# Value rounds issued in pairs, with fifteen probability slots, in a two-block transformer kernel

## What is computed

```
q = q * cos + rotate_half(q) * sin
k = k * cos + rotate_half(k) * sin
scores = einsum('bhgtd,bhkd->bhgtk', qg, k) / sqrt(16)
scores = where(causal, scores, min)
attn = softmax(scores)
ctx = einsum('bhgtk,bhkd->bhgtd', attn, v)
```

## Time and profile before

| | |
|---|---|
| median of three runs | 753.19 us |
| the profiled execution | 752.28 us |
| its span, first to last instruction | 750.5 us |
| TensorE (PE) busy | 707.6 us, 94% |
| VectorE (DVE) busy | 480.8 us, 64% |
| ScalarE (ACT) busy | 314.7 us, 42% |
| GpSimd (POOL) busy | 313.8 us, 42% |
| heads 0 to 7 of the attention | 84.9 to 324 us |

### The profile page before, as it was taken

One profiled execution on the slowest core, in us unless ns is written; L12 is line 12 of the kernel. 1 busy time (PEld: TensorE's weight loads), 2 busy tenths in 40 slices (PEclk: granted clock), 3 DMA queues, 4 the chain that ended last, 5 costly groups with the idle time before them and its releaser, 6 DMA issues.

```text
span 750.5 us, 10313 instructions
## 1 busy us (share of the span) xinstructions
PE 707.6 (94%) x3718; PEld 429.5 (57%) x3718; DVE 480.8 (64%) x722; ACT 314.7 (42%) x530; POOL 313.8 (42%) x254
## 2 busy tenths in 40 slices
PE   4998899999999998999999999999789999999998
PEld 1444343334333332366778888555357888877886
DVE  3787778788888887439675468768785432337211
ACT  3311367677676667732335211554243323223100
POOL 0325673866665568803366233216422212216300
PEclk9999999999999999999999999999889999999999
DMA  8347516264171100120133100231010111012111
GB/s 301 116 127 223 125 44 166 74 123 72 55 190 35 24 3 2 61 76 23 29 84 98 43 1 0 81 66 48 29 41 0 57 56 56 28 57 63 36 70 43
DMA packets 24111, 53.00 MB, mean 71 GB/s; under 512 B 4252, under 2 KB 8100, under 8 KB 23044
## 3 DMA queue, kind: packets, MB, share of 16 engines
q1 hardware_dynamic: 24068, 52.44, 25.1%
HBM read 45.63 MB, written 6.60 MB: 70 GB/s over the span
## 4 chain that ended last, share of the span: by engine, by line
PE 75%; DVE 14%; issue 5%; POOL 2%; DMA 2%; SPq 1%; ACT 1%; DVEq 0%; POOLq 0%; ACTq 0%
PE ps L895 72%; DVE mxp L1869 3%; DVE st L1711 1%; DMA rq<-in_mask 1%; PE ps L912 1%; DVE xnb L1735 1%; DVE x L1956 1%; DVE x L2069 1%; PE ps L1081 1%; DVE rt L1750 1%; POOL pr L2310 1%; DVE dg L2103 0%; ACT pr L1516 0%; PE ps L1088 0%; DVE qsw L1920 0%
## 5 line engine op out<-in xcount | busy, mean ns | idle before, releaser
L895 PE MATMUL ps<-arena 128*128 128x512 f32 (+1 forms) x1404 | 327.2, 392 | 1.2 <-POOL arena L2416 0.5
L895 PEld LDWEIGHTS ps<-arena 128*128 128x128 f32 (+1 forms) x1404 | 259.9, 186 | 60.8 <-issue 1.7
L1869 DVE TENSOR_REDUCE mxp<-ps 128x2 f32<-128x1024 f32 (+3 forms) x160 | 172.5, 1114 | 40.2 <-PE ps L895 39.6
L1516 ACT ACTIVATE pr<-ps 128x512 f32<-128x512 f32 x288 | 161.3, 597 | 73.7 <-PE ps L895 69.7
L895 PE MATMUL ps<-Kst,Qst 96*128 96x512 bf16 (+3 forms) x384 | 97.0, 330 | 5.4 <-DVE mxp L1869 4.2
L895 PE MATMUL ps<-Qst,Kst 99*128 99x512 bf16 x288 | 96.1, 385 | 1.8 <-ACT pr L1516 1.4
L2310 POOL TENSOR_TENSOR pr<-pr,cap 128x512 int32<-128x512 int32 x56 | 70.2, 1269 | 38.4 <-ACT pr L1516 38.4
L895 PE MATMUL ps<-pr,vr 128*32 128x512 f32 x576 | 76.7, 604 | 1.4 <-POOL pr L2310 1.4
L895 PEld LDWEIGHTS ps<-Kst,Qst 96*128 96x128 bf16 x384 | 35.8, 98 | 50.6 <-DVE mxp L1869 20.9
L895 PEld LDWEIGHTS ps<-Qst,Kst 99*128 99x128 bf16 x288 | 24.6, 97 | 64.3 <-ACT pr L1516 45.8
L2416 POOL TENSOR_TENSOR arena<-raw,arena 128x1024 fp32r<-128x1024 f32 x11 | 26.7, 2431 | 80.1 <-ACT arena L1589 80.1
(11 more groups left out here) (205 smaller groups left out, 842.6 us busy)
## 6 DMA issues: line engine op xcount, KB each, us to landing
wmr<-in_wmr SPq DMA_DIRECT2D x8, 1280.0 KB, 11.1
raw<-in_w SPq DMA_DIRECT2D x16, 512.0 KB, 3.3
Qst<-q_parts SPq DMA_DIRECT2D x42, 128.0 KB
q_parts<-qparts SPq DMA_DIRECT2D x3, 768.0 KB, 4.6
x<-in_x SPq DMA_DIRECT2D x8, 256.0 KB, 5.9
wm<-in_wm SPq DMA_DIRECT2D x4, 512.0 KB, 7.3
raw<-in_up SPq DMA_DIRECT2D x8, 256.0 KB, 2.6
raw<-in_down SPq DMA_DIRECT2D x8, 256.0 KB, 2.5
```

The costliest lines, as they stand in the source:

```text
L895: return nc.tensor.matmul(outp, lhs, rhs, start=start, stop=stop, skip_group_check=True)
L1516: A(pr[:, k % PRING, :], ps[:, t_bank(n, k), :], ACT.Exp, scale=float(DH) ** -0.5).then_inc(exp_done, 1)
L1869: V.tensor_reduce(mxp[:, kh, g0:g0 + heads, i].rearrange("p (b e) -> p b e", e=per), units, AXX, ALU.max)\
```

## The change

In heads 0 to 6 the rounds 0 to 7 are issued two at a time: rounds 0 and 1 behind unit 11, 2 and 3 behind 19, 4 and 5 behind 27, 6 and 7 behind 35. Round 8 stays behind unit 1 of the next head. The last head keeps its order. The places of all units, score units, `max_turn`, `mod_step` and `ctx_turn` in the list stay as they are.

The ring gets 15 slots (13 in head 0, because slots 13 and 14 lie where the third rotary piece of the queries is read until head 0). A table says which slot each unit uses and which unit used it before; each exponential waits for the round of that unit. The first exponential of head 1 also waits for `part_q` to reach 3, the end of the rotary work. `ot` stays where it was.

```diff
-PRING = 12
-assert NTU % PRING == 0 and NTU == 4 * ROUNDS
+PRING = 15
+assert NTU == 4 * ROUNDS
+FIRST_PRING = 13
+def ring_table():
+    slots, held, user = {}, {}, {}
+    for n in range(NKV):
+        for k in range(NTU):
+            s = k % FIRST_PRING if n == 0 else (NTU + (n - 1) * NTU + k - NTU // FIRST_PRING * FIRST_PRING) % PRING
+            slots[n, k], user[n, k] = s, held.get(s)
+            held[s] = n * NTU + k
+    return slots, user
+PSLOT, PUSER = ring_table()
...
-        pr = at("pr", [P, PRING, D], F32, HT_B)
-        ot = at("ot", [P, 2, D], F32, HT_B + PRING * 2048)
+        pr = [at(f"pr{s}", [P, D], F32, HT_B + 2048 * s) for s in range(12)]
+        pr += [at("pr12", [P, D], F32, WR_B + 12800), at("pr13", [P, D], F32, ACT_B + 76 * 1024),
+               at("pr14", [P, D], F32, ACT_B + 78 * 1024)]
+        ot = at("ot", [P, 2, D], F32, HT_B + 12 * 2048)
...
                     t_unit(n, k)
-                    if k % 4 == 3 and k > 4:
-                        pv_round(n, k // 4 - 1)
+                    if k % 8 == 3 and k > 4:
+                        for r in range(2):
+                            pv_round(n, k // 4 - 2 + r)
                     if k == 1 and n:
                         pv_round(n - 1, ROUNDS - 1)
...
                     act.wait_ge(t_full, n * NTU + k + 1)
-                    if k >= PRING or n:
-                        act.wait_ge(pv_done, n * ROUNDS + (k - PRING) // 4 + 1)
-                    A(pr[:, k % PRING, :], ps[:, t_bank(n, k), :], ACT.Exp, scale=float(DH) ** -0.5).then_inc(exp_done, 1)
+                    if n == 1 and k == 0:
+                        act.wait_ge(part_q, 3)
+                    if PUSER[n, k] is not None:
+                        act.wait_ge(pv_done, PUSER[n, k] // 4 + 1)
+                    A(pr[PSLOT[n, k]][:, :], ps[:, t_bank(n, k), :], ACT.Exp, scale=float(DH) ** -0.5).then_inc(exp_done, 1)
```

More of the change, by code:

```diff
@@ L1069, in pv_round @@
                     q = 32 * strip(i)
-                    last = mm(ps[q:q + 32, 6 + i // 4, :], vr[:, j, :], pr[:, k % PRING, :], j == FIRST_J[i],
+                    last = mm(ps[q:q + 32, 6 + i // 4, :], vr[:, j, :], pr[PSLOT[n, k]][:, :], j == FIRST_J[i],
                               j == LAST_J[i])
@@ L2308, in mask_round @@
                     pool.wait_ge(exp_done, n * NTU + k + 1)
-                    v = pr[:, k % PRING, :].rearrange("p (g t) -> p g t", g=G).bitcast(I32)
+                    v = pr[PSLOT[n, k]][:, :].rearrange("p (g t) -> p g t", g=G).bitcast(I32)
                     nc.gpsimd.tensor_tensor(v, v, cap[:, :].unsqueeze(1).to_broadcast([P, G, P]), ALU.mult).then_inc(masked, 1)
```

## The result

| | before | after |
|---|---|---|
| median, five runs each | 753.19 us (752.57 to 754.71) | 767.08 us (764.77 to 767.47) |
| ratio | | 1.018, 95% interval 1.016 to 1.020 |
| the profiled execution | 752.28 us | 766.93 us |
| its span | 750.5 us | 765.1 us |

The change makes the kernel 13.9 us slower. The forecast was 768.5 us, its range 762.5 to 773.

The account below looks back on a forecast made before the run. TensorE bounds, busy 94% of the span. Head 0 +3.4, heads 1 to 4 +8.8, head 5 +1.3, head 6 +1.8 sum to +15.3 us: 768.5 us on the median of 753.19, range 762.5 to 773.

Parts of the forecast that it names:

- its rivals: Only the border saved, 748.4 us, 5%; no change, 3%; VectorE waits hidden, 757.2, 7%; border saves nothing, 773.3, 10%.
- The new waits: Behind units 7, 15, 23 and 31 TensorE waits 0.63, 0.56, 1.10 and 0.60 us: 2.89 in a head.
- The border: Between a pair's two rounds TensorE saves 0.17 us, 0.68 in a head, 4.8 over 28 pairs.
- The rival in which the border saves nothing: The second round of a pair waits for its weights or the first to drain: 773.3 us, chance 10%.
- Head 0: First head: +1.8 us from waits less borders, plus 1.6 for `nm` held by GpSimd, together +3.4.
- The hold: In head 0 `nm` would start inside a GpSimd operation and end with it: +1.6 us, bounds 0 and 1.6.
- two precedents: In the earlier traces a CAST (107.77 to 109.09) and an `nm` of 1.00 us each ended with GpSimd's operation.
- its rule: Trainium skill: GpSimd shares SBUF interfaces with VectorE, and instructions with two SBUF inputs contend there; gives head 0's 1.6 us.
- The stall of 0.81: Head 5's context transposes wait for VectorE; the pair before nearly removes this, -0.9 us, so head 5 costs +1.3.
- Head 6: Costs +1.8 us: 2.21, less 0.20 for the wait behind unit 31, less 0.25 for GpSimd's effect on `nm`.
- the 0.81 of the earlier trace: In head 6 `max_turn` loses 0.81 us to GpSimd before the change; forecast change -0.8 to +0.3, taken as -0.25.
- The edits at nothing: Ring slots, GpSimd masks, the wait on `part_q`, value copies and DMAs were claimed to cost no time.

Follow-up runs that it names:

- One place given back: Changed kernel with round 4 back behind unit 23 and round 5 behind 27, three pairs left in heads 0 to 6: 760.0 us, ratio 1.0088.
- Work put into the places: Changed kernel with three more matmuls of 512 columns behind units 7, 15, 23 and 31 of heads 0 to 6: 767.73 us, ratio 1.0193.
- the run without the GpSimd hold: Changed kernel with GpSimd's last 1024-column rotary operation cut into four of 256 columns: 766.34 us, ratio 1.0189.
- The run with 12 slots: Kernel before, with its ring of 12 slots, and its rounds issued in pairs: 765.65 us, ratio 1.0168.
- the run with the ring alone: Changed kernel with its table of 15 slots, but single rounds behind every fourth unit as before: 753.11 us, ratio 0.9999.
- Half the reductions: Kernels before and after, VectorE's score reductions reading half of the columns, exponentials at scale 0: 743.57 us (from before) and 751.99 us (from after).
- the second: Changed kernel with VectorE's score reductions over half of the columns and exponentials at scale 0: 751.99 us, ratio 0.9986.

## Why the prediction was right

**The mechanism.** It was the one forecast: in four places of each head TensorE comes 1.09 us sooner to work that isn't ready. The experiments separate it from its rivals. The ring is free. The pairs make the loss without it. One place given back returns its own price. Work put into the places is nearly free. The part that the experiments don't settle is the fall of the clock in head 0, 1.4 of the 14.7 us.

**The new waits.** In head 3 the forecast had unit 8 0.41 behind unit 7 and unit 9 0.66 behind that; the rows say 0.42 and 0.65. The score unit behind unit 15 was to be 0.56 late; it is 0.57, at 201.01 and so 0.79 behind unit 15 at 200.22, where 0.22 would do. At units 24, 25 and the transpose the sum was 1.10 and is 1.10, and the transpose stands 1.85 behind unit 23, as said. Behind unit 31 it was 0.60, and is 0.60 (215.16 is 0.82 behind 214.34). With 0.05 us for every release, read off one place of the chain, no wait is off by more than 0.02.

**The border.** Here a size was off. The forecast took 0.17, the way out of one round and into the next, and called it the most, "since a strip's passes can't overlap themselves". It is 2.09 - 1.86 = 0.23. The 0.17 wasn't the most: what the sum left out is that the passes of the second round come 0.43 behind each other where the second pass of a single round comes 0.46 behind the first (0.45 at 197.25). Over 28 pairs that is 6.5 in place of 4.8 us. The rival in which the border saves nothing is excluded. This term alone takes 1.7 us off the forecast, and the middle heads, 1.97 in place of 2.21, are off by just it.

**Head 0.** By its own terms it comes to 1.8 - 0.24 of more border = 1.56, and the run without the GpSimd hold has 1.55. The hold was to cost 1.6 and costs 1.93 - 0.19 = 1.74: `nm` started at 107.20, forecast at 107.22. That makes 3.3. The other 1.4 of the 4.67 was not forecast: it is the fall of the clock behind the idle 2.13 us. The run with 12 slots has the hold, 1.31 of it, and no fall: +2.81, and 1.55 + 1.31 is 2.86. The forecast priced a wait by its length. It left out that the clock can fall at a long one. That the idle time is the cause isn't shown. With the hold, two profiled runs in which TensorE idled for 2.07 and 2.13 us have the fall, and four in which it idled for 0.77 to 1.70 don't; but the clock fell in head 6 of another run without such a gap. The forecast also took two precedents for the hold, and only `nm` has the two SBUF inputs that its rule names: the CAST reads one tile.

**Head 5.** The stall of 0.81 is gone, and the head costs 1.13: 1.97 - 0.81 = 1.16.

**Head 6.** Forecast 1.8, measured 0.93. `nm` there is back to 0.19, at 305.65, so the 0.81 of the earlier trace rows came back in full; the forecast had taken the middle of -0.8 and +0.3. The wait behind unit 31, estimated at 0.4, is 0.37, so 1.97 - 0.23 - 0.81 gives 0.93. The lower end of the bounds was right, by little: `nm` started 0.07 ahead of the next GpSimd operation (305.72). In the run with GpSimd's operation in quarters, whose head 6 has the same list, a lower clock took back more than this.

**The sum.** 1.7 less by the border and 0.6 less by head 6 stand against 1.4 more by the clock in head 0: 15.3 against 14.67 us. That the total came so near owes something to this cancelling; without the clock's part it would have been 13.3 and 766.5 us. The range held the result with room, but its upper end wasn't the sum of its terms: 768.5 + 4.8 for the border + 0.55 for head 6 is 773.9, and 28 waits of 0.1 more make it 776.7, not 773.

**The edits at nothing.** They are at nothing: the run with the ring alone has the time of the kernel before, and after, the value rounds wait for GpSimd's masks for the same 1.4 us in all as before.

**What stays open.** Which runs have the fall in head 0, and what brings it. The five runs of after lie between 764.77 and 767.47, and only one is profiled. Their mean clocks are 0.984 to 0.991, the fastest run having the highest, so the 1.4 us may not be in all of them. Half the reductions put the two kernels 8.4 us apart by their medians and 7.0 by their profiled runs, of which the heads hold 6.3. The ten runs of the second spread from 749.96 to 754.45 us, and the profiled one, of 750.54, is among the short ones.

## What to carry over

Work that the bounding engine does anyway is also the time in which the others catch up. Before two pieces of it are put together, look at what follows each place that it leaves, and take from the timeline when the producer of that ends. A cover taken away costs what it covered, once for every place, and a wait that you remove may have another right behind it. Small saves at the borders, 0.23 us here, were outweighed in every order that was tried; moving the order behind along took back two thirds of the loss and no more.

## What the runs showed of the hardware

- Passes of back-to-back f32 value rounds follow each other by 0.43 us; the first two passes of a round by 0.45 or 0.46. The way into a round costs 0.09, and the unit behind it starts 0.54 behind its last pass. Two rounds together save 0.23.
- A VectorE operation of 0.19 us with its operands in SBUF took 1.50 and 1.93 us where it started inside a 2.1 us GpSimd operation, and ended with it, but 0.19 where it started 0.21 ahead of it. With GpSimd's operation in quarters it took 0.20, started 0.15 ahead of a piece's end. The Trainium skill (GPSIMD Engine Reference, section Specifications) has the shared SBUF interfaces, and these rows agree. They show the length of the hold too: up to the end of GpSimd's operation. A CAST with one SBUF input was held in the same way, 1.47 in place of 0.21.
- TensorE's granted clock went to its lower level at an idle 2.13 us in head 0, and behind an idle 2.07 in another run. In a third it fell behind a stretch with no gap over 0.5, 3.23 us busy in 4, where the same stretch of after kept its clock. The first and the third fall cost 1.4 and 1.6 us, more than the waits of any one of the four places.
